# Small discarded TensorE products in the unrolled first steps of an attention and conditional-convolution kernel

## The reference, cut to what matters

```python
x = x + attention(group_norm(x))
#   qkv = w_qkv @ rmsnorm(x); q: softmax over the 32 features of a head
#   k: softmax over the 1024 pixels and 4 memory columns
#   context = k @ v.T per head; out = rmsnorm(w_out @ (context @ q) + b)
x = x + condconv(group_norm(x))
#   r = sigmoid(relu(fc(relu(rconv(pooled x)))))
#   w[b] = sum over k of r[b, k] * expert_weight[k];  3x3 convolution of image b with w[b]
```

## Time and profile before

| | |
|---|---|
| median of 3 runs | 474.91 us (473.31 to 475.17) |
| the profiled execution | 477.94 us, of which 476.2 us lie between its first and last instruction |
| TensorE, matmul busy | 434.6 us, 91% |
| VectorE, ScalarE, GpSimd busy | 364.4, 292.3, 240.4 us (77%, 61%, 50%) |
| mean granted TensorE clock | 0.961 |

### The profile page before, as it was taken

How to read it: one execution, slowest core, us unless ns; L and a number is a source line. 1 busy time by engine, 2 the same in 40 slices (tenths; PEclk the granted TensorE clock), 3 DMA queues, 4 the chain that set the end, 5 groups by cost and what they waited for, 6 DMA issues and landing times.

```text
span 476.2 us, 8406 instructions
## 1 busy us (share of the span) xinstructions
PE 434.6 (91%) x2414; PEld 373.7 (78%) x2414; DVE 364.4 (77%) x769; ACT 292.3 (61%) x859; POOL 240.4 (50%) x229
## 2 busy tenths in 40 slices
PE   2759675999999999999999999999999999998976
PEld 1648464798989888888888888889898888886765
DVE  3251588779898989898898989898989798888500
ACT  2445658295867675867768494858676858653211
POOL 4412347565737374655654565637373755425220
PEclk9976979599999999999999999999999999999979
DMA  7302024240708070614334251608080605144411
GB/s 214 129 0 90 1 88 178 88 179 26 283 1 310 1 285 26 239 72 167 145 133 176 97 211 62 246 4 304 0 310 1 234 33 192 74 152 159 176 45 44
DMA packets 18785, 61.60 MB, mean 129 GB/s; under 512 B 2992, under 2 KB 4032, under 8 KB 18752
## 3 DMA queue, kind: packets, MB, share of 16 engines
q1 hardware_dynamic: 18752, 61.21, 34.2%
HBM read 19.29 MB, written 8.39 MB: 58 GB/s over the span
## 4 chain that ended last, share of the span: by engine, by line
PE 71%; DVE 10%; issue 8%; ACT 5%; POOL 3%; DMA 1%; POOLq 1%; DVEq 0%; ACTq 0%
PE ps_conv L1170 31%; PE ps_att L1108 8%; PE ps_y L1134 6%; PE ps_qkv L1088 4%; PE ps_qkv L1075 4%; PE ps_qkv L1090 4%; PE ps_qkv L1089 3%; PE ps_qkv L1124 3%; PE ps_y L1140 2%; PE ps_att L1106 2%; DVE w_full L961 1%; PE ps_stat L1147 1%; ACT expert_raw L618 1%; DVE k_exp L789 1%; ACT k_exp L573 1%
## 5 line engine op out<-in xcount | busy, mean ns | idle before, releaser
L565 ACT ACTIVATE qkv<-ps_qkv,scale 128x384 f32<-128x384 f32 x128 | 70.6, 595 | 14.1 <-PE ps_qkv L1090 11.4
L506 POOL TENSOR_TENSOR w_lo<-w_full,w_hi 128x1152 fp32r<-128x1152 f32 x16 | 42.5, 2654 | 56.9 <-ACT w_hi L624 29.9
L479 POOL TENSOR_TENSOR q_exp<-q_exp,q_rsum 128x1024 f32<-128x1024 f32 x16 | 30.6, 1915 | 78.9 <-DVE q_rsum L818 78.9
L577 ACT ACTIVATE q_exp<-q_exp 128x1024 f32<-128x1024 f32 x16 | 17.0, 1061 | 63.7 <-DVE q_exp L804 63.7
L1088 PE MATMUL ps_qkv<-wqkv_hi,x_hi 128*128 128x384 f32 x128 | 46.9, 366 | 5.3 <-ACT qkv L565 4.8
L1090 PE MATMUL ps_qkv<-wqkv_hi,x_lo 128*128 128x384 f32 x128 | 44.7, 349 | 0.0
L1089 PE MATMUL ps_qkv<-wqkv_lo,x_hi 128*128 128x384 f32 x128 | 44.5, 348 | 0.0
L1170 PE MATMUL ps_conv<-img_hi,w_hi 128*128 128x512 f32 x96 | 38.7, 403 | 5.1 <-POOL w_lo L506 5.1
L589 ACT ACTIVATE q_t<-ps_qkv 128x512 f32<-128x512 f32 x32 | 19.1, 596 | 39.4 <-PE ps_qkv L1124 39.4
L1170 PE MATMUL ps_conv<-right_lo,w_hi 128*128 128x512 f32 (+1 forms) x96 | 41.6, 433 | 0.0
L469 POOL TENSOR_TENSOR x_lo<-x,x_hi 128x1024 fp32r<-128x1024 f32 x16 | 38.0, 2373 | 6.4 <-ACT x_hi L554 6.4
(11 more groups left out here) (138 smaller groups left out, 1240.6 us busy)
## 6 DMA issues: line engine op xcount, KB each, us to landing
xa<-in_x_dram SPq DMA_DIRECT2D x16, 512.0 KB, 3.8
xb<-in_x_dram SPq DMA_DIRECT2D x16, 512.0 KB, 4.5
out_dram<-expert_raw SPq DMA_DIRECT2D x16, 512.0 KB, 2.8
left_hi<-img_hi SPq DMA_DIRECT2D x16, 511.5 KB, 3.0
right_hi<-img_hi SPq DMA_DIRECT2D x16, 511.5 KB, 3.7
left_lo<-img_lo SPq DMA_DIRECT2D x16, 511.5 KB, 4.1
right_lo<-img_lo SPq DMA_DIRECT2D x16, 511.5 KB, 4.8
expert_raw<-_conv_expert_weight_dram SPq DMA_DIRECT2D x1, 1728.0 KB, 9.4
```

The lines of the kernel that those rows point to most:

```text
L479: nc.gpsimd.tensor_tensor(q_exp[:, :, :], q_exp[:, :, :], q_rsum[:, :].unsqueeze(2).to_broadcast((128, NT * HEADS, DH)), ALU.mult).then_in ...
L506: nc.gpsimd.tensor_tensor(w_lo[p][:, :, :].rearrange("p t o -> p (t o)"), w_full[:, :], w_hi[p][:, :, :].bitcast(F32).rearrange("p t o -> ...
L565: nc.scalar.activation(qkv[:, t, 0:QKV], ps_qkv[t % 2][:, 0:QKV], ACT.Copy, scale=scale1[:, t:t + 1]).then_inc(qkv_done, 1)
```

## The change

A table `IDLE_PRODUCTS` and a function `keep_busy(t, place)` are added to TensorE's program. At six places of `step`, for the steps named in the table and for no others, it issues a number of products of `ones` (128 x 128) with 64 columns of `ones` into `ps_conv[1]`. Nothing reads them, and no semaphore counts them. In step -1 they wait for `pool_zeros`; in steps 2 and 3, at every place but `expert_transposes`, for the ScalarE copies of the expert tiles, which have been done by then.

```diff
+            IDLE_PRODUCTS = {"group_means": {-1: 12, 1: 24}, "project": {2: 10, 3: 6}, "k_part_transpose": {1: 14, 2: 14, 3: 20},
+                             "k_shift": {1: 7}, "expert_transposes": {2: 9}, "contexts": {3: 22}}
+
+            def keep_busy(t, place):
+
+                if not isinstance(t, int) or t not in IDLE_PRODUCTS[place]:
+                    return
+                if t < 0:
+                    pe.wait_ge(pool_zeros, 1)
+                if t >= 2 and place != "expert_transposes":
+                    pe.wait_ge(experts_ready, EXPERT_FILLS)
+                for _ in range(IDLE_PRODUCTS[place][t]):
+                    mm(ps_conv[1][:, 0:64], ones[:, :], ones[:, 0:64], start=True, stop=True)
...
                 conv(6)
+                keep_busy(t, "expert_transposes")
                 if isinstance(t, int) and t == 2:
                     expert_transposes()
                 conv(4)
+                keep_busy(t, "contexts")
                 do(contexts, t, p, 2)
...
                 do(context_transpose, t, p, 2)
+                keep_busy(t, "group_means")
                 turn(group_means, t, p, 0)
...
                 conv(3)
+                keep_busy(t, "project")
                 do(project, t, p, 1, 2)
...
                 conv(14)
+                keep_busy(t, "k_part_transpose")
                 do(k_part_transpose, t, p, 1)
                 conv(2)
                 do(y_transpose, t, p, 2)
                 conv(1)
+                keep_busy(t, "k_shift")
                 do(k_shift, t, p, 1)
```

## The result

| | before | after |
|---|---|---|
| median | 475.04 us (473.31 to 477.86, 4 runs) | 481.62 us (481.28 to 482.03, 4 runs) |
| ratio, 95% interval | | 1.0133 (1.0083 to 1.0183) |
| profiled execution | 477.94 us, span 476.2 us | 481.46 us, span 479.7 us |
| mean granted clock | 0.961 | 0.993 |
| TensorE busy | 434.6 us, 91% | 459.1 us, 96% |

The account below looks back on a forecast made before the run. TensorE was taken as the bound from 94.5 us on, with waits and 1.2 GHz stretches before. Terms 2.0 - 1.5 - 1.8 - 1.8 - 3.0 = -6.1 us, scaled from the profiled 477.94 to the median, gave 468.8 us, range 465.5 to 473.0.

Parts of the forecast that it names:

- 24 products of step 1: Ahead of step 1's group means: 5.6 us of products, clock rising after two thirds; +2.0 us net, ends -0.9 and +5.4.
- 12 products of step -1: Ahead of step -1's group means, while TensorE waits for the first image: 3.2 us that fit there, costing nothing.
- Experts -1.5: Expert transposes of image 0: at 2.4 GHz ScalarE's copies wait less; -1.5 us, ends 0 and -2.1.
- contexts of image 0 -1.8: Image 0's contexts: from 4.21 to 2.40 us at the higher clock; -1.8 us, ends 0 and -1.8.
- first rival: Clock falls in the expert transposes, so image 0's contexts run at 1.2 GHz: 3.3 us less gain, 471.6 us; chance 0.28.
- 22 products and the contexts of image 1, -1.8: Ahead of image 1's contexts: products overrun by 0.2 us, contexts gain 2.0; -1.8 us, ends -0.1 and -2.0.
- 10 ahead of `project`: Ahead of `project`'s third group, in a wait for ScalarE: 1.6 us of products, costing nothing.
- second rival: Products at 0.25 us each run over the idle places: 5.6 us less gain, 474.4 us, no change; chance 0.10.
- Step 4, -3.0: Convolution and image 2's contexts: start 1.0 us sooner after a new wait, contexts 2.0 us shorter; -3.0 us, ends 0 and -3.1.
- slower rival: Small products do not hold the clock, 0.50 at 63 us despite 22 products: +6.9 us, 481.8 us; chance 0.05.
- stretch in which transposes alone held the clock: From 67.3 to 70.6 us, TensorE nearly all transposes, busy 2.97 of 3.30 us: granted clock stayed at 1.00.

Follow-up runs that it names:

- e1_no_group_means: The changed kernel without the 12 and 24 products ahead of the group means in steps -1 and 1; 470.71 us, ratio 0.9977.
- the version that fits: The changed kernel with no products ahead of the group means and the other counts cut to the idle places at 0.22 us each; 468.30 us, ratio 0.9904.
- second and third trace of before: Two more traced executions of the kernel before, with no edit; 475.65 and 470.39 us.
- e9_bare_experts: The version that fits, without its 6 products ahead of `k_shift` and 9 ahead of the expert transposes; 470.80 us, ratio 0.9968.

## Why the prediction was wrong, step by step

**The 24 products of step 1: the step that failed.** The prediction took 0.27 us a product at 1.2 GHz, let the clock rise after two thirds of them, and came to +2.0 us. Measured: 0.43 us each (10.3 us for 24, start to start), no rise in 10.3 us, and the first copy of image 0's projections 9.5 us late, of which 8.5 are these products: beyond even the stated end of +5.4. Three things in it were wrong. The price was read by moving columns ("64 columns are half of 130"), while it went by the weights' side, which is 128 columns whatever moves: 128 moving columns cost the same 0.11 us a matmul at 2.4 GHz, 32 weight columns 0.06. The right row was at hand, the sixteen matmuls with 130 columns at 0.124 us each: it had been set down as an upper bound and lies 13% above the value. Second, the rise of the clock after two thirds was the author's assumption, made because the engine would be without gaps; three traces show 10.3 us of these products without a rise, and the clock comes up only behind them, at 33.0 us in the first trace and between 28 and 29.4 in the second, by the distances of the projections' matmuls. Without the products it comes up in the same projections (24.4 us in `e1_no_group_means`). Third, what gain was to come back in step 1 (1.8 us, from transposes and projections at 2.4 GHz) went with it.

**The 12 products of step -1.** They last until 6.95 and push image 0's group means from 5.99 to 6.95. That 1.0 us is part of the 9.5, and was costed at nothing; with 0.43 us each, 12 were 5.2 us, not 3.2.

**Experts -1.5, contexts of image 0 -1.8.** Measured between the stations of the table: -1.7 and -1.8. Of the 1.7, 0.5 came ahead of the experts, where the last projections of step 1 already ran at 2.4 GHz (the exponential of k ends 8.96 us late, at 42.48 for 33.52), and 1.2 in the expert transposes. Right in kind and nearly in size. That the clock held through the thin expert transposes goes with the 16 products ahead of them (1.00 from 36 to 60 us in the trace after): in the traces with shorter ones (0.50 from 38 to 44 us) or without (0.50 from 32 to 37) it fell, so the first rival was a live one.

**22 products and the contexts of image 1, -1.8.** The contexts went from 4.4 to 2.4 us, as forecast; the products overran by 1.7 us instead of 0.2, so that 0.3 us was left. Here the forecast again failed by the price, 0.22 for 0.16 us. The 10 ahead of `project` overran by 0.3. The second rival, the products run over the idle places, had these right in kind, with 0.25 us a product.

**Step 4, -3.0.** Measured: -2.8 (6.07 late to 3.24). The new wait of 1.1 us for the exponential is there, as named.

**The slower rival** gave 481.8 us, near the measured 481.6, but not by its mechanism: it needed a clock that stays at 1.2 GHz in the 22 products, and the clock stayed up. It got 5% for being slower, and the part that really was slower, products at 1.2 GHz ahead of all of step 1's work, stood in the forecast as +2.0.

**The base.** The sum was made against the longest of all executions seen. Its 1.8 us for image 0's contexts are to be had in that trace alone, and the 2.0 us for image 2's in two of the three. Of the gains of 8.1 us that the trace promised, the version that fits gives 4.1 us on the median.

**The transposes and the clock.** Against its first rival the prediction set, as a stretch in which transposes alone held the clock. That row was weaker than it was said to be: 17 of its 26 matmuls are transposes, with products between them. The later traces go further: in the second and third trace of before and in `e9_bare_experts` the granted clock, 0.50 from 34 to 37 us, went to 1.00 between 37.5 and 38.4, ahead of the contexts (from 38.67, 38.94 and 38.28), with nothing but transposes having run since about 30 us. So in three traces the clock came up with this kernel's float32 transposes alone.

**A sum.** In the second rival, 24 products at two thirds 0.40 and one third 0.25 us are 8.4 us, 2.8 more than the forecast's 5.6 and not 2.2; its time would be 475.0 us instead of 474.4. Nothing else hangs on it.

Open: why the 64-column products did not raise the clock at 1.2 GHz when they held it at 2.4 GHz, where the clock did come up in 128-column ones of the same price (by the end of step -1's in two traces, and ahead of step 1 in one). The runs show that it is so, not why.

## What to carry to other kernels

A product put in to hold the clock is work on the critical engine, so count it at a price measured for its own shape and at the clock it will meet (here 128 weight columns cost 0.11 us a matmul at 2.4 GHz and 32 cost 0.06), and never put more of it ahead of a piece of work than that piece waits anyway; where the clock was still down, it cost 0.43 instead of 0.22 us here, and with 64 columns it did not raise the clock in 10.3 us. Before costing a lower clock from one trace, look how far the executions spread: a trace at the upper end promises gains that the median doesn't have. And when two rows bound an unknown price, ask which resource sets each, rather than interpolate by the one size that differs.

## What the runs showed of the hardware that was not expected

- In a dense row, a float32 matmul with 128 weight columns took 0.11 us at 2.4 GHz and 0.21 us at 1.2 GHz, with 64 as with 128 moving columns; with 32 weight columns and 64 moving ones it took 0.06 and 0.11 us.
- 48 such matmuls with 64 columns, back to back for 10.3 us, left the clock at 1.2 GHz in all three traces of them, while it came up on the way in the one trace with the same number of 128 columns. Once up, the 64-column ones held it, 44 at a time for 5 us.
- In these traces the record gave 1.00 for stretches in which the distances between matmuls were those of 1.2 GHz (0.32 us for 384 columns, up to 32.9 us in the changed kernel), as long as it had not yet shown a first fall; a mean granted clock of 0.993 for the changed kernel hides some 30 us of them.
- Executions of the kernel before spread over 7.8 us (470.1 to 477.9) with a middle of 302.64 to 302.71 us in three traces. All the rest lies ahead of it and behind it, where the clock falls and rises at other moments in each trace; with the waits filled, the last two too, six executions spread over 2.0 us.
